# Moving SBUF tensors by multiples of 32 bytes in a cross-attention kernel

## The chip, the cores and the metric

The kernel runs on one core of a Trainium2 chip. The metric is the device time of one execution in microseconds (us). Three runs of the kernel before took 325.67 to 325.92 us, with a median of 325.76 us.

## The reference

```python
def ref(x, ctx, mask, Wq, Wk, Wv, Wo, gamma, beta):   # H = 8, D = 256, B = 8
    Q = (x @ Wq).reshape(B, -1, H, D).transpose(0, 2, 1, 3)        # x    8 x 256 x 256
    K = (ctx @ Wk).reshape(B, -1, H, D).transpose(0, 2, 1, 3)      # ctx  8 x 256 x 192
    V = (ctx @ Wv).reshape(B, -1, H, D).transpose(0, 2, 1, 3)
    score = einsum('bhqd,bhkd->bhqk', Q, K) / sqrt(D)
    attn = softmax(where(mask != 0, score, -inf))
    c = einsum('bhqk,bhkd->bqhd', attn, V).reshape(B, -1, H * D)
    out = c @ Wo + x
    return layernorm(out) * gamma + beta                            # eps 1e-5
```

## The kernel before, in words

The weights are folded once: A = Wq Wk^T and C = Wv Wo for each head (`fold_A`, `fold_C`, L316 to L355), so that a head costs only g = A^T x, scores = g^T ctx, t = ctx^T probs and out = t^T C. Context has 192 features, a lower part of 128 (L) and an upper part of 64 (U); the upper parts of two heads are packed into one tile.

Float32 accuracy comes from splitting every operand into a hi and a lo part, both `float32r`; each product is hi hi + hi lo + lo hi. All these matrix products go through `split_products` (L309 to L314), one `matmul` for each pair (stationary, moving). So each matmul on TensorE has two operands in SBUF, the stationary one, which a weight load brings in, and the moving one, which streams past. In the trace a matmul is written out<-moving,stationary.

The work is a pipeline of 32 steps (8 batches of 4 pairs of heads, `t` counts them). In `step` (L489 to L500) TensorE does four stages in this order:

- `scores(t)`: 20 matmuls, stationary `gL_hi`, `gL_lo`, `gU`, moving `ctxT_hi`, `ctxT_lo`, 256 columns each
- `query_products(t+1)`: 18 matmuls, stationary `A_hi`, `A_lo`, moving `xT_hi`, `xT_lo`, 256 columns
- `output_products(t-4)`: 18 matmuls, stationary `tL_hi`, `tL_lo`, `tU_hi`, `tU_lo`, moving `CL_hi`, `CL_lo`, `CU_hi`, `CU_lo`, 256 columns
- `context_products(t-3)`: 10 matmuls, stationary `ctxL_hi`, `ctxL_lo`, `ctxU`, moving `pT_hi`, `pT_lo`, 512 columns

ScalarE (ACT) makes the hi parts and the exponentials, VectorE (DVE) the lo parts of g and t, the maxima, the 32 x 32 transposes and the layer norm (its steps with j = 3 and j = 0 are the fullest, because add_residual, statistics, centre and normalise fall there), and GpSimd (POOL) divides the probabilities and makes the lo part of `pT`. The order on each engine is written out by hand; every dependence is a semaphore. The last steps differ: for `t` = 30, `places` (L125) puts the split t into tiles that are free by then, `xT_hi` and `xT_lo` as the lower stationary part and `gU` as the upper one.

SBUF tensors are allocated in the order of the `sb(...)` calls, one behind the other, each at the next address in a partition that is a multiple of 32 bytes. The first four (`wq_raw` to `wo_raw`) start at 16,512, a multiple of 128. All large tensors are multiples of 128 bytes long, so a start modulo 128 (the residue) is moved only by the small tensors that stand ahead: those of 8 or 16 bytes each take 32 bytes. Start addresses modulo 128 in the kernel before, and in the order that the change gives (worked out by this rule):

```
tensors                            before  changed
A_hi, A_lo                            0       0
gL_hi, gL_lo, gU                     64       0
tL_hi, tL_lo, tU_hi, tU_lo           32       0
ctxL_hi, ctxL_lo, ctxU               64      64
xT_hi, xT_lo, ctxT_hi, ctxT_lo       64      64
CL_hi, CL_lo, CU_hi, CU_lo            0      64
pT_hi, pT_lo (both buffers)          32      64
gamma, beta, ident, zeros             0      64
xT_raw, ctxT_raw, ctx_raw, mask*     64      64
x_res, neg_scores                    64      64
probs (both buffers)                 96      64
squares, pT_raw, tU_moved, tU        32      64
y, y_scaled, y_out                   32      64
```

All slices that a matmul takes start a multiple of 128 bytes behind the tensor's start, so these residues are those of the operands.

Of the kernel before, what the change touches and what calls it, by code (L numbers as in the profile page):

```python
# [8 lines left out]
F32R = mybir.dt.float32r  # L9
# [4 lines left out]
P = 128  # L14
B = 8
S = 256
KV = 256
# [7 lines left out]
UP = DL - P  # L25
PAIRS = H // 2
STEPS = B * PAIRS
QT = S // P
KT = KV // P
IT = DI // P  # L30
# [10 lines left out]
def attention_kernel(nc, xT, x, ctxT, ctx, mask, wqT, wkT, wvT, wo, gamma, beta, out, scratch):  # L41
    es = ExitStack()
    with es:
        def sb(name, shape, dt=F32):
            return es.enter_context(nc.sbuf_tensor(name, shape, dt))
# [11 lines left out]

        A_hi = sb("A_hi", [P, IT, PAIRS * PW], F32R)
        A_lo = sb("A_lo", [P, IT, PAIRS * PW], F32R)
        CL_hi = sb("CL_hi", [P, H, DI], F32R)  # L60
        CL_lo = sb("CL_lo", [P, H, DI], F32R)
        CU_hi = sb("CU_hi", [P, PAIRS, DI], F32R)
        CU_lo = sb("CU_lo", [P, PAIRS, DI], F32R)
        gamma_sb = sb("gamma_sb", [P, DI])
        beta_sb = sb("beta_sb", [P, DI])
        ident = sb("ident", [P, P])
        zeros = sb("zeros", [P, DI])
        eps_col = sb("eps_col", [P, QT])
        power_col = sb("power_col", [P, QT])

        xT_raw = sb("xT_raw", [P, IT, S])
        xT_hi = sb("xT_hi", [P, IT, S], F32R)
        xT_lo = sb("xT_lo", [P, IT, S], F32R)
        ctxT_raw = sb("ctxT_raw", [P, 2, KV])
        ctxT_hi = sb("ctxT_hi", [P, 2, KV], F32R)
        ctxT_lo = sb("ctxT_lo", [P, 2, KV], F32R)
        ctx_raw = sb("ctx_raw", [P, KT, DL])
        ctxL_hi = sb("ctxL_hi", [P, KT, P], F32R)
        ctxL_lo = sb("ctxL_lo", [P, KT, P], F32R)
        ctxU = sb("ctxU", [P, KT, 2 * UP], F32R)  # L80
        mask_raw = sb("mask_raw", [P, KV], I32)
        mask_low = sb("mask_low", [P, KV])
        mask_bias = sb("mask_bias", [P, KV])
        x_res = sb("x_res", [P, QT, DI])

        gL_hi = sb("gL_hi", [P, 2, S], F32R)
        gL_lo = sb("gL_lo", [P, 2, S], F32R)
        gU = sb("gU", [P, 2, S], F32R)
        neg_scores = sb("neg_scores", [P, 2 * QT, KV])
        neg_max = sb("neg_max", [P, 2 * QT])  # L90
        probs = [sb(f"probs{n}", [P, 2 * QT, KV]) for n in range(2)]
        row_sum = sb("row_sum", [P, 2 * QT])
        inv_sum = sb("inv_sum", [P, 2 * QT])
        squares = sb("squares", [P, SQUARES, 2 * QT, SQ])
        pT_raw = [sb(f"pT_raw{n}", [P, KT, ROWS, 2 * QT, SQ]) for n in range(2)]
        pT_hi = [sb(f"pT_hi{n}", [P, KT, 2, S], F32R) for n in range(2)]
        pT_lo = [sb(f"pT_lo{n}", [P, KT, 2, S], F32R) for n in range(2)]
        tL_hi = sb("tL_hi", [P, 2, S], F32R)
        tL_lo = sb("tL_lo", [P, 2, S], F32R)
        tU_moved = sb("tU_moved", [P, S])  # L100
        tU = sb("tU", [P, S])
        tU_hi = sb("tU_hi", [P, S], F32R)
        tU_lo = sb("tU_lo", [P, S], F32R)

        y = sb("y", [P, QT, DI])
        y_scaled = sb("y_scaled", [P, QT, DI])
        y_out = sb("y_out", [P, QT, DI])
        stats = sb("stats", [P, QT, 6])
        mean_var = sb("mean_var", [P, QT, 2])
        var_eps = sb("var_eps", [P, QT])  # L110
        rstd = sb("rstd", [P, QT])

# [999 lines left out]
```

How the kernel before makes its waits and increments, by code:

```python
        @block.sync  # L202
# [17 lines left out]
            def store_out(b):  # L220
                sp.wait_ge(y_out_done, QT * b + QT)
                sp.dma_start(batch_of(out, b), y_out[:]).then_inc(out_stored, 16)
# [24 lines left out]
            def load_ahead(b):  # L248
                sp.wait_ge(xT_split, b)
                load_xT(b)
                sp.wait_ge(ctxT_split, b)
                load_ctxT(b)
                sp.wait_ge(mask_lowered, b)
                load_mask(b)
# [1 line left out]
            def load_ctx_ahead(b):  # L257
                sp.wait_ge(ctx_split, 2 * b)
                load_ctx(b)
# [1 line left out]
            def load_residual(b):  # L262
                sp.wait_ge(out_bank_read, b + 1)
                load_x_res(b)
# [1 line left out]
            def carry_squares(t, j, raw_free=True):  # L267
                sp.wait_ge(squares_done, 2 * t + 2)
                sp.dma_start(scratch[j].rearrange("i c k jj r -> (i c) (k jj r)"),
                             squares[:].rearrange("p s n r -> p (s n r)")).then_inc(squares_stored, 16)
                sp.wait_ge(squares_stored, 16 * t + 16)
                if raw_free:
                    sp.wait_ge(pT_split, 2 * (t - 2) + 2)
                for jj in range(ROWS):
                    sp.dma_start(pT_raw[j % 2][SQ * jj:SQ * (jj + 1)].rearrange("c k i n r -> c k i (n r)"),
                                 scratch[j][:, :, :, jj, :].rearrange("i c k r -> c k i r")).then_inc(pT_in[j % 2], 16)
# [23 lines left out]
                sp.dma_start(out[B - 1][:, q, :], y_out[:, q, :]).then_inc(out_stored, 16)  # L303
            sp.wait_ge(out_stored, 16 * (B + QT))
```

## Time and profile before

| what | value |
|---|---|
| median of 3 runs | 325.76 us |
| the profiled execution's own time | 325.59 us |
| its span in the trace | 323.8 us |
| TensorE busy | 315.3 us, 97% |
| VectorE busy | 253.2 us, 78% |
| ScalarE busy | 222.4 us, 69% |
| GpSimd busy | 181.2 us, 56% |
| granted TensorE clock | full in all 40 slices |

How to read it: a span is the time from the first to the last instruction in the trace; the device time is longer by what lies around it. PE is TensorE's matmuls, PEld its weight loads. A matmul's recorded duration overlaps with the next one's, so what a matmul costs in a row of them is the distance from its start to the next one's start.

### The profile page before, as it was taken

The page shows a single profiled execution, that of the slowest core. Times are in us where ns is not written, and L with a number is a line of the kernel's source. Part 1 is how long each engine was busy: PE and PEld are TensorE (multiplying, and loading weights), DVE is VectorE, ACT ScalarE, POOL GpSimd, SP SyncE. Part 2 cuts the span into 40 slices and gives each one's busy share as a digit, 9 for nine tenths or more (in the row PEclk, how much of TensorE's full clock was granted, in tenths as well). Part 3 has the DMA queues.
Part 4 walks back from the last instruction along what each step waited for, and adds up shares of the span by engine and source line. Part 5 has one row for each costly group of instructions (what it writes and reads, how often), then busy time and mean ns, then how long its engine had stood idle before and what let it go on. Part 6 is the DMA issues. An engine that isn't in the chain of part 4 may idle for free.

```text
span 323.8 us, 7403 instructions
## 1 busy us (share of the span) xinstructions
PE 315.3 (97%) x2264; PEld 293.9 (91%) x2264; DVE 253.2 (78%) x721; ACT 222.4 (69%) x601; POOL 181.2 (56%) x183
## 2 busy tenths in 40 slices
PE   8999998999999999999999999999999999999992
PEld 6898887999999999999999999999999999998982
DVE  0457868777999779977997879977997789975685
ACT  2456668768867787668776797668766887777640
POOL 1122358457864487557855486548755686447211
PEclk9999999999999999999999999999999999999999
DMA  7995533464345453463345435364356525440100
GB/s 260 361 408 195 139 124 131 155 210 133 95 134 190 164 175 118 144 232 131 130 136 204 154 130 165 128 208 145 113 180 173 192 83 175 157 136 2 34 32 32
DMA packets 46910, 50.26 MB, mean 155 GB/s; under 512 B 3504, under 2 KB 37040, under 8 KB 46896
## 3 DMA queue, kind: packets, MB, share of 16 engines
q1 hardware_dynamic: 46608, 49.56, 46.0%
q10 hardware_dynamic: 288, 0.52, 0.6%
q8 instruction: 7, 0.11, 0.2%
q14 instruction: 7, 0.06, 0.1%
HBM read 32.24 MB, written 17.83 MB: 155 GB/s over the span
## 4 chain that ended last, share of the span: by engine, by line
PE 89%; DVE 3%; POOL 2%; DMA 2%; ACT 1%; issue 1%; SPq 1%; POOLq 0%; DVEq 0%
PE score_bank L312 23%; PE out_bank L312 19%; PE gL_bank L312 13%; PE tL_bank L312 13%; PE tU_bank L312 8%; PE gU_bank L312 7%; DMA wq_raw<-in_wqT 2%; PE tL_bank L346 1%; PE spare_bank L346 1%; PE tL_bank L328 1%; PE tU_bank L328 1%; POOL pT_lo L1016 1%; DVE tU L815 1%; PE tU_bank L352 1%; PE spare_bank L312 1%
## 5 line engine op out<-in xcount | busy, mean ns | idle before, releaser
L993 POOL TENSOR_TENSOR probs<-probs,inv_sum 128x512 f32<-128x512 f32 x64 | 66.8, 1044 | 87.8 <-DVE inv_sum L778 87.1
L590 ACT ACTIVATE probs<-neg_scores,neg_max 128x256 f32<-128x256 f32 x128 | 64.3, 504 | 31.8 <-DVE neg_max L767 31.7
L1016 POOL TENSOR_TENSOR pT_lo<-pT_raw,pT_hi 128x512 fp32r<-128x512 f32 x60 | 76.6, 1299 | 11.6 <-ACT pT_hi L547 11.6
L767 DVE CUSTOM_DVE_ANT_0 neg_scores<-score_bank,mask_bias 128x256 f32<-128x256 f32 x128 | 49.1, 420 | 7.4 <-PE score_bank L312 4.5
L547 ACT ACTIVATE tL_hi<-tL_bank 128x512 fp32r<-128x512 f32 x31 | 18.5, 598 | 38.4 <-PE tL_bank L312 38.4
L788 DVE STREAM_TRANSPOSE squares<-probs 128x512 f32<-128x512 f32 x60 | 42.3, 706 | 0.3
L715 DVE TENSOR_TENSOR tL_lo<-tL_bank,tL_hi 128x512 fp32r<-128x512 f32 x31 | 21.3, 687 | 23.2 <-ACT tL_hi L547 23.1
L312 PE MATMUL score_bank<-ctxT_hi,gU 128*128 128x256 f32 x128 | 36.5, 285 | 0.7 <-POOL ctxT_lo L1005 0.7
L312 PE MATMUL score_bank<-ctxT_hi,gL_lo 128*128 128x256 f32 x128 | 36.3, 283 | 0.0
L312 PE MATMUL score_bank<-ctxT_lo,gL_hi 128*128 128x256 f32 x128 | 36.2, 283 | 0.0
L312 PE MATMUL score_bank<-ctxT_hi,gL_hi 128*128 128x256 f32 x128 | 36.2, 283 | 0.0
L312 PE MATMUL score_bank<-ctxT_lo,gU 128*128 128x256 f32 x128 | 36.0, 281 | 0.0
L312 PE MATMUL gL_bank<-xT_hi,A_lo 128*128 128x256 f32 x128 | 35.4, 276 | 0.0
L312 PE MATMUL gL_bank<-xT_hi,A_hi 128*128 128x256 f32 x128 | 35.3, 276 | 0.0
L312 PE MATMUL gL_bank<-xT_lo,A_hi 128*128 128x256 f32 x128 | 35.3, 276 | 0.0
L547 ACT ACTIVATE pT_hi<-pT_raw 128x512 fp32r<-128x512 f32 x60 | 34.3, 622 | 0.0
L312 PE MATMUL out_bank<-CL_hi,tL_lo 128*128 128x256 f32 x118 | 33.3, 283 | 0.0
L312 PE MATMUL out_bank<-CL_lo,tL_hi 128*128 128x256 f32 x118 | 33.3, 282 | 0.0
L312 PE MATMUL out_bank<-CL_hi,tL_hi 128*128 128x256 f32 x118 | 33.1, 280 | 0.0
L715 DVE TENSOR_TENSOR gU<-gU_bank,gU 64x256 fp32r<-64x256 f32 x64 | 27.0, 422 | 2.1
L312 PEld LDWEIGHTS score_bank<-ctxT_hi,gU 128*128 128x128 f32 x128 | 24.3, 190 | 3.8 <-POOL ctxT_lo L1005 1.4
L815 DVE TENSOR_TENSOR tU<-tU_bank,tU_moved 64x256 f32<-64x256 f32 x62 | 26.0, 419 | 1.6 <-ACT tU_moved L631 0.6
(166 smaller groups left out, 949.7 us busy)
## 6 DMA issues: line engine op xcount, KB each, us to landing
scratch<-squares SPq DMA_DIRECT2D x30, 512.0 KB, 2.6
pT_raw<-scratch SPq DMA_DIRECT2D x120, 128.0 KB, 3.1
xT_raw<-in_xT SPq DMA_DIRECT2D x8, 256.0 KB, 4.4
ctxT_raw<-in_ctxT SPq DMA_DIRECT2D x8, 256.0 KB, 4.6
wo_raw<-in_wo SPq DMA_DIRECT2D x4, 512.0 KB, 13.9
x_res<-in_x SPq DMA_DIRECT2D x8, 256.0 KB, 3.2
out<-y_out SPq DMA_DIRECT2D x7, 256.0 KB, 2.7
wq_raw<-in_wqT SPq DMA_DIRECT2D x3, 512.0 KB, 7.4
```

The costliest lines, as they stand in the source:

```text
L312: ins = nc.tensor.matmul(into, stationary, moving, start=first and n == 0, stop=last and n == len(pairs) - 1, skip_group_check=shared)
L328: ins = nc.tensor.matmul(dst[:, i * DL:(i + 1) * DL], wq_raw[:, h * DT + d, i * P:(i + 1) * P], wk_raw[:, h * DT + d, :], start=d == 0, st ...
L346: ins = nc.tensor.matmul(lower[:, hh, :], wv_raw[:, h * DT + d, 0:P], wo_raw[:, h * DT + d, :], start=d == 0, stop=d == DT - 1)
L352: ins = nc.tensor.matmul(upper[hh * UP:(hh + 1) * UP, 0, :], wv_raw[:, h * DT + d, P:DL], wo_raw[:, h * DT + d, :], start=d == 0, stop=d = ...
L547: return nc.scalar.activation(dst, src, ACT.Copy)
L590: nc.scalar.activation(probs[j % 2][:, n, :], neg_scores[:, n, :], ACT.Exp, bias=neg_max[:, n:n + 1], scale=-1.0, accum_out=row_sum[:, n:n ...
L715: return nc.vector.tensor_tensor(dst, whole, hi.bitcast(F32), ALU.subtract)
L767: nc.vector.tensor_tensor_reduce(out=neg_scores[:, n, :], in0=score_bank[hh][:, q, :], in1=mask_bias[:], scale=-SCALE, scalar=3.0e38, op0= ...
L788: nc.vector.transpose(squares[:, :, rows, :].rearrange("p s n c -> p n s c"), probs[j % 2][:, rows, :].rearrange("p n (s c) -> p n s c", c ...
L815: nc.vector.tensor_tensor(tU[part, :], places("tU", t)[0][part, hh, :], tU_moved[part, :], ALU.add).then_inc(tU_summed, 1)
L993: nc.gpsimd.tensor_tensor(probs[j % 2][:, rows, :], probs[j % 2][:, rows, :], inv, ALU.mult) \
L1016: nc.gpsimd.tensor_tensor(pT_lo[j % 2][:, k].rearrange("p hh (q i r) -> p (hh q) i r", q=QT, i=ROWS), pT_raw[j % 2][:, k].rearrange("p i n ...
```

## The change

Only the order of the `sb(...)` calls changes; shapes, types, instructions, their order and their semaphores stay as they are.

```diff
         A_hi = sb("A_hi", [P, IT, PAIRS * PW], F32R)
         A_lo = sb("A_lo", [P, IT, PAIRS * PW], F32R)
+        gL_hi = sb("gL_hi", [P, 2, S], F32R)
+        gL_lo = sb("gL_lo", [P, 2, S], F32R)
+        gU = sb("gU", [P, 2, S], F32R)
+        tL_hi = sb("tL_hi", [P, 2, S], F32R)
+        tL_lo = sb("tL_lo", [P, 2, S], F32R)
+        tU_hi = sb("tU_hi", [P, S], F32R)
+        tU_lo = sb("tU_lo", [P, S], F32R)
+
+        eps_col = sb("eps_col", [P, QT])
+        power_col = sb("power_col", [P, QT])
+
+        ctxL_hi = sb("ctxL_hi", [P, KT, P], F32R)
+        ctxL_lo = sb("ctxL_lo", [P, KT, P], F32R)
+        ctxU = sb("ctxU", [P, KT, 2 * UP], F32R)
+
+        xT_hi = sb("xT_hi", [P, IT, S], F32R)
+        xT_lo = sb("xT_lo", [P, IT, S], F32R)
+        ctxT_hi = sb("ctxT_hi", [P, 2, KV], F32R)
+        ctxT_lo = sb("ctxT_lo", [P, 2, KV], F32R)
         CL_hi = sb("CL_hi", [P, H, DI], F32R)
         CL_lo = sb("CL_lo", [P, H, DI], F32R)
         CU_hi = sb("CU_hi", [P, PAIRS, DI], F32R)
         CU_lo = sb("CU_lo", [P, PAIRS, DI], F32R)
+        pT_hi = [sb(f"pT_hi{n}", [P, KT, 2, S], F32R) for n in range(2)]
+        pT_lo = [sb(f"pT_lo{n}", [P, KT, 2, S], F32R) for n in range(2)]
+
         gamma_sb = sb("gamma_sb", [P, DI])
         beta_sb = sb("beta_sb", [P, DI])
         ident = sb("ident", [P, P])
         zeros = sb("zeros", [P, DI])
-        eps_col = sb("eps_col", [P, QT])
-        power_col = sb("power_col", [P, QT])
...
         mean_var = sb("mean_var", [P, QT, 2])
+        neg_max = sb("neg_max", [P, 2 * QT])
+        row_sum = sb("row_sum", [P, 2 * QT])
+        inv_sum = sb("inv_sum", [P, 2 * QT])
         var_eps = sb("var_eps", [P, QT])
         rstd = sb("rstd", [P, QT])
```

The lines that are left out take each tensor that was moved away from its old place; `neg_max`, `row_sum` and `inv_sum` stood between `neg_scores`, `probs` and `squares`.

## Rows read from the trace of the kernel before

**Rows 1.** The page: span, TensorE's busy share, its granted clock in 40 slices.

```profile
span 323.8 us, 7403 instructions
...
PE 315.3 (97%) x2264; PEld 293.9 (91%) x2264; DVE 253.2 (78%) x721; ACT 222.4 (69%) x601; POOL 181.2 (56%) x183
...
PEclk9999999999999999999999999999999999999999
```

**Rows 2.** Chain of work that ended last, one step: start us, us, what.

```profile
195.51 2.39 PE score_bank L312 x20
197.90 0.68 PE gU_bank L312 x6
198.58 1.36 PE gL_bank L312 x12
199.94 2.16 PE out_bank L312 x18
202.10 0.94 PE tL_bank L312 x4
203.03 0.47 PE tU_bank L312 x2
...
204.43 2.39 PE score_bank L312 x20
```

**Rows 3.** Waits from 52 to 294 us: total us, times, longest.

```profile
PE score_bank L312 <- POOL ctxT_lo L1005: 0.7, 1, 0.7
```

**Rows 4.** TensorE's groups, each shape apart: busy us, mean ns of one.

```profile
L312 PE MATMUL score_bank<-ctxT_hi,gU 128*128 128x256 f32 x128 | 36.5, 285 | 0.7 <-POOL ctxT_lo L1005 0.7
...
L312 PE MATMUL gL_bank<-xT_hi,A_hi 128*128 128x256 f32 x128 | 35.3, 276 | 0.0
...
L312 PE MATMUL out_bank<-CL_hi,tL_lo 128*128 128x256 f32 x118 | 33.3, 283 | 0.0
...
L312 PE MATMUL tL_bank<-pT_hi,ctxL_hi 128*128 128x512 f32 x62 | 24.9, 401 | 0.2 <-issue 0.2
```

**Rows 5.** Timeline of TensorE near the end: start us, us, matmul.

```profile
301.41 0.28 PE L312 MATMUL spare_bank<-CL_lo,tL_hi 128*128 128x256 f32 x1
...
302.60 0.28 PE L312 MATMUL out_bank<-CL_hi,tL_lo 128*128 128x256 f32 x1
...
313.47 0.28 PE L312 MATMUL spare_bank<-CL_hi,xT_hi 128*128 128x256 f32 x1
...
315.39 0.28 PE L312 MATMUL out_bank<-CU_hi,gU 128*128 128x256 f32 x1
```

**Rows 6.** Busy time of each engine in steps j=3 and j=0 (us, instructions).

```profile
186.40:204.30 17.90, 17.90 (x134) 16.96 (x133) 15.86 (x46) 13.70 (x38) 13.83 (x15) 1.00 0.43 143
```

**Rows 7.** Timeline of VectorE over steps j=3 and j=0: start us, us, instruction.

```profile
187.02 0.69 DVE L715 TENSOR_TENSOR tL_lo<-tL_bank,tL_hi 128x512 fp32r<-128x512 f32 x1 [1.39 <-ACT tL_hi L547]
187.97 0.42 DVE L767 CUSTOM_DVE_ANT_0 neg_scores<-score_bank,mask_bias 128x256 f32<-128x256 f32 x1 [0.25 <-PE score_bank L312]
...
203.26 0.69 DVE L715 TENSOR_TENSOR gL_lo<-gL_bank,gL_hi 128x512 fp32r<-128x512 f32 x1
...
205.36 0.68 DVE L715 TENSOR_TENSOR tL_lo<-tL_bank,tL_hi 128x512 fp32r<-128x512 f32 x1
```

**Rows 8.** Timeline of TensorE: the first matmul that reads the lo part from rows 7.

```profile
204.75 0.28 PE L312 MATMUL score_bank<-ctxT_hi,gL_lo 128*128 128x256 f32 x1
```

**Rows 9.** Chain of work that ended last, the first steps.

```profile
19.24 2.60 PE score_bank L312 x20
...
34.04 2.59 PE score_bank L312 x20
...
49.06 2.05 POOL probs L993 x2
```

**Rows 10.** Chain of work that ended last, the end.

```profile
305.02 0.60 ACT tL_hi L547
...
316.13 1.36 PE spare_bank L312 x9
```

More of the change, by code:

```diff
@@ L67, in attention_kernel @@
         zeros = sb("zeros", [P, DI])
-        eps_col = sb("eps_col", [P, QT])
-        power_col = sb("power_col", [P, QT])
         xT_raw = sb("xT_raw", [P, IT, S])
-        xT_hi = sb("xT_hi", [P, IT, S], F32R)
-        xT_lo = sb("xT_lo", [P, IT, S], F32R)
         ctxT_raw = sb("ctxT_raw", [P, 2, KV])
-        ctxT_hi = sb("ctxT_hi", [P, 2, KV], F32R)
-        ctxT_lo = sb("ctxT_lo", [P, 2, KV], F32R)
         ctx_raw = sb("ctx_raw", [P, KT, DL])
-        ctxL_hi = sb("ctxL_hi", [P, KT, P], F32R)
-        ctxL_lo = sb("ctxL_lo", [P, KT, P], F32R)
-        ctxU = sb("ctxU", [P, KT, 2 * UP], F32R)
         mask_raw = sb("mask_raw", [P, KV], I32)
@@ L84, in attention_kernel @@
         x_res = sb("x_res", [P, QT, DI])
-        gL_hi = sb("gL_hi", [P, 2, S], F32R)
-        gL_lo = sb("gL_lo", [P, 2, S], F32R)
-        gU = sb("gU", [P, 2, S], F32R)
         neg_scores = sb("neg_scores", [P, 2 * QT, KV])
-        neg_max = sb("neg_max", [P, 2 * QT])
         probs = [sb(f"probs{n}", [P, 2 * QT, KV]) for n in range(2)]
-        row_sum = sb("row_sum", [P, 2 * QT])
-        inv_sum = sb("inv_sum", [P, 2 * QT])
         squares = sb("squares", [P, SQUARES, 2 * QT, SQ])
         pT_raw = [sb(f"pT_raw{n}", [P, KT, ROWS, 2 * QT, SQ]) for n in range(2)]
[L96 to L99, printed above, removed]
         tU_moved = sb("tU_moved", [P, S])
         tU = sb("tU", [P, S])
-        tU_hi = sb("tU_hi", [P, S], F32R)
-        tU_lo = sb("tU_lo", [P, S], F32R)
         y = sb("y", [P, QT, DI])
```

## The prediction

> **What bounds the kernel now.** I read the page first: TensorE is busy 97% of the span at the full granted clock in every slice, 2.4 GHz, the higher of its two levels [rows 1]. Busy TensorE is not proof of a bound, so the chain of waits came next. From 52 to 294 us it is TensorE alone: one step is 20 score matmuls in 2.39 us, 6 + 12 query matmuls in 2.04, 18 output matmuls in 2.16 and 10 context matmuls from 202.10 to 204.43, 2.33, together 8.92 us [rows 2]. Then the waits: in this stretch TensorE waited 0.7 us once, at its start, and never again [rows 3]. So nothing but the distance from one matmul to the next sets 27 steps of the pipeline (t = 4 to 30), about 241 us. A change that touches no instruction can matter only through that distance.
>
> **What the distance depends on now.** Each stage divided by its count gives ns per matmul: scores 2.39/20 = 119.5, query 2.04/18 = 113.3, output 2.16/18 = 120, context 2.33/10 = 233 for twice the columns [rows 2]. Three stages have the same shape, yet one is 6 to 7 ns faster; the mean durations say the same, 285 and 283 against 276 ns [rows 4]. Put the residues of the SBUF map beside it: query has stationary 0, moving 64 (64 apart), scores 64 and 64 (0 apart), output 32 and 0 (32 apart), context 64 and 32 (32 apart). That may be the stage and not the address, so I looked for one stage with two addresses. The end has it: for t = 30 the split t lies in `xT` and `gU` at residue 64, with C at 0 as always. Those output matmuls, 17 distances from 313.47 to 315.39, take 113 ns; the same form with `tL` at 32, 10 distances from 301.41 to 302.60, takes 119 [rows 5]. Same helper, shape, moving tiles and banks, another stationary address. I take it that 64 apart is the fast case whichever of the two stands at 0, and that 0 and 32 apart both cost 6 to 7 ns at 256 columns.
>
> One rule speaks against all of this. The Trainium skill (TensorE: Matmul & The Clock Gate, Step-by-step: what each phase is for) says that TensorE reads its moving operand and its weights through two independent ports, so that loading the next weights takes nothing from the running matmul. By it addresses would not matter and the sum would be zero, 325.8 us; by the rows above it is not. The trace disagrees with it by those 6 to 7 ns [rows 2, 5].
>
> **The change part by part.**
>
> Scores go from 0 to 64 apart (stationary 0, moving 64: just what query has). 20 x 113.3 ns = 2.27 us against 2.39: -0.12 a step.
>
> Output goes from 32 to 64 apart, again 0 and 64: 18 x 113.3 = 2.04 against 2.16: -0.12 a step.
>
> Query keeps 0 and 64: nothing.
>
> Context goes from 32 apart (stationary 64, moving 32) to 0 apart, both at 64. No row shows 512 columns at 0 or 64 apart, so I bound it. Below: an undisturbed 256-column matmul takes 113.3 ns and 256 further columns at 2.4 GHz 106.7, so 220 ns, 2.20 us a step (-0.13). Above: twice a score matmul at 0 apart, 2 x 120 = 240, 2.40 us (+0.07). Inside: 220 plus the 6.7 ns that 0 apart costs the scores is 226.7; twice the fast query matmul is also 226.7. I take that, 2.27 us, -0.06 a step. Unchanged at 233 is a serious alternative, since at 256 columns 0 and 32 apart cost the same.
>
> The other tiles: `ident` and `zeros` move from 0 to 64, for 16 transposes and the warming only, nothing to speak of. The operands of GpSimd's lo part of `pT` were at one residue (32) and are again (64). Several ScalarE and VectorE operands change residue (`probs` 96 to 64, `squares` 32 to 64, `tU` stays away from its hi part by 64 instead of 0). The trace shows no price for that on these engines; what hides it is the slack before TensorE's waits, below. DMA destinations shift likewise, under the same cover.
>
> Step: 8.92 - 0.12 - 0.12 - 0.06 = 8.62 us, -0.30.
>
> **Does it all lie on the path?** Steps 4 to 30: 27 x 0.30 = 8.1 us. Before them the chain holds the scores of t = 0 to 2 but then goes through GpSimd (pT lo, ctx, probs) until 52 us [rows 9]: 3 x 0.12 = 0.36 saved, and the scores of t = 3 hidden. After them, t = 31: scores 0.12, 30 output matmuls ahead of 305 us at 6.7 ns = 0.20, two context blocks 0.12; at 305.02 the chain passes to ScalarE and VectorE until 316.13, when TensorE has 9 last output matmuls [rows 10], 0.06. In the stretch between, 12 matmuls with `xT` as stationary become 0 apart and lose 12 x 6.7 = 0.08 us, but TensorE is not what the chain follows there; uncovered it would cost that 0.08. Sum 8.1 + 0.36 + 0.44 + 0.06 = 9.0 us. Against the profiled execution's own 325.59 that is 316.6; the median is 0.17 above that execution, so **316.8 us**.
>
> **Do the others keep up?** The fullest pair of steps for VectorE is j = 3 and j = 0: 15.86 us busy in 17.90 [rows 6]. From its tL_lo at 187.02 to the one at 205.36 it takes 18.34 us, with three waits inside of 0.25 to 0.29 (the first is shown), 0.82 in all, so 17.5 us without waiting [rows 7]. The pair will last 2 x 8.62 = 17.24. So VectorE comes out of it up to 0.3 us late, and catches up in the next two steps, each of which has some 2 us of room. What TensorE waits for there is gL_lo: done at 203.26 + 0.69 = 203.95, first read at 204.75, so 0.80 us early [rows 7, 8]. Even if none of VectorE's waits shrank, that becomes 0.80 - 0.60 - 0.03 = 0.17; if they all do, up to 0.99. Close, but no wait. ScalarE and GpSimd, 13.70 and 13.83 us in the pair [rows 6], are further away.
>
> **Rivals.**
>
> *Context takes another value.* At 233 ns, unchanged: 9.0 less 29 x 0.06 = 7.3 us saved, 318.5. At 240: 29 x 0.07 more is lost, 320.5. At 220: 29 x 0.07 more is gained, 314.8. For unchanged speaks the equality of 0 and 32 at 256 columns; for 220 speaks that its moving tile comes from 32 to a start like the fast stages', so that part of what it pays now may belong to the start and not to the distance.
>
> *VectorE becomes the bound* in the fullest pairs, because its instructions are slower at their new addresses or its late pair does not recover. Then a pair lasts 17.5 instead of 17.24, or with the order's gaps about 17.6: 7 pairs x 0.36 = 2.5 us given back, 319.3. Against: the slack of gL_lo, and that TensorE waits on nothing now. It decides from 0.17 to 0.99 us of growth over some 16 us of VectorE work, 1 to 6%.
>
> *Nothing changes*, 325.8: the 6 to 7 ns belong to the stage and the case at the end is an accident. This is the rule of the ports named above. Against: it would have to explain 113 and 119 ns for one form of instruction [rows 5].
>
> *Slower*: context at one residue collides on every access of the weight load and not once a matmul. The rest gains 7.3 us, and some 290 context matmuls are on the path, so it decides from 7.3/290 = 25 ns each, 258 instead of 233. At 265 ns: 327.8 us. Against: the scores are at 0 apart too and pay 7 ns, for as many weights; the load does not grow with the columns.
>
> **How the numbers follow.** Forecast, context near 227 and the rest as reckoned: 0.45, own range 315.6 to 317.7. Context unchanged up to 240, 317.7 to 320.5: 0.22. Context toward 220, 314.4 to 315.6: 0.14. VectorE as bound, about 319.3: 0.08. No change: 0.05. Slower: 0.04. Left over: 0.02. From 314.5 to 320.5 about 0.87 is held. I keep that range because its ends are the bounds of the context price. A measurement of this kernel can tell about 0.2%, 0.65 us, from no change; all cases but the last three are faster than that: faster 0.90, same 0.06, slower 0.04.
>
> **What will show it.** In the chain of the changed kernel a step should read scores 2.27, query 2.04, output 2.04, context 2.27, step starts 8.62 apart. Score and output groups should have a mean of 276 ns, as query. The 12 matmuls on `xT` near the end should rise from 113 to 120 ns: the one place where the change makes a pair worse, and so the check on the mechanism. No new wait of TensorE before 294 us, and gL_lo still ahead of its reader in steps j = 0. I am wrong if scores or output stay at 119 ns, if context leaves 220 to 240, or if TensorE begins to wait for VectorE.

## The result, and the profile after

The changed kernel takes 325.05 us (median of 18 runs, 324.65 to 325.78), the kernel before 325.81 us (18 runs, 325.59 to 326.13): a ratio of 0.9977, 95% interval 0.9970 to 0.9984. It is faster, but by 0.76 us, where 9 were forecast. The mean granted clock is 0.999 in both profiled executions. For two experiments (e9 and e13, below) single runs are told, since they fall into groups 8 to 10 us apart at the same granted clock (0.995 to 1.000), and that is the finding.

The page of the changed kernel: span, TensorE's busy share, its granted clock.

```profile
span 322.8 us, 7403 instructions
...
PE 313.6 (97%) x2264; PEld 293.2 (91%) x2264; DVE 253.1 (78%) x721; ACT 222.2 (69%) x601; POOL 181.0 (56%) x183
...
PEclk9999999999999999999999999999999999999999
```

TensorE still sets the time and waits as rarely as in [rows 3]; its waits from 52 to 294 us:

```profile
PE score_bank L314 <- POOL ctxT_lo L1007: 0.7, 1, 0.7
```

Two steps of the chain of work that ended last (start us, us, what), against [rows 2]:

```profile
61.56 2.27 PE score_bank L314 x20
63.82 0.68 PE gU_bank L314 x6
64.50 1.36 PE gL_bank L314 x12
65.86 2.04 PE out_bank L314 x18
67.90 0.93 PE tL_bank L314 x4
...
70.19 2.35 PE score_bank L314 x20
72.55 0.71 PE gU_bank L314 x6
73.26 1.41 PE gL_bank L314 x12
74.67 2.12 PE out_bank L314 x18
76.79 0.93 PE tL_bank L314 x4
...
79.10 0.94 PE score_bank L314 x8
```

These two steps do the same work with the same addresses. (`gU_bank` and `gL_bank` are the two parts of query.) The first, from 61.56, is the forecast step: scores 2.27, query 2.04, output 2.04, 8.63 us in all. The second, from 70.19, has scores 2.35 (2.36 by the matmuls' starts), query 0.71 + 1.41 = 2.12, output 2.12, together 8.91, and all later steps are like it. Query, whose residues did not change, went from 113.3 to 117.7 ns a matmul. Context takes 2.31 us in the second kind of step and 2.29 in the first, where [rows 2] have 2.33.

The groups of TensorE (busy us, mean ns of one), against [rows 4]:

```profile
L314 PE MATMUL score_bank<-ctxT_hi,gU 128*128 128x256 f32 x128 | 36.3, 283 | 0.7 <-POOL ctxT_lo L1007 0.7
L314 PE MATMUL gL_bank<-xT_hi,A_hi 128*128 128x256 f32 x128 | 35.8, 280 | 0.0
...
L314 PE MATMUL out_bank<-CL_hi,tL_lo 128*128 128x256 f32 x118 | 32.9, 279 | 0.0
L314 PE MATMUL tL_bank<-pT_hi,ctxL_hi 128*128 128x512 f32 x62 | 24.6, 398 | 0.3 <-issue 0.3
```

Scores fell from 285 to 283 ns here and output from 283 to 279, but query rose from 276 to 280. Near the end, the 12 output matmuls with `xT` as the stationary part, which are now 0 apart, were to rise from 113 to 120 ns. Nine distances of the timeline (start us, us, matmul), against [rows 5]:

```profile
312.68 0.28 PE L314 MATMUL spare_bank<-CL_hi,xT_hi 128*128 128x256 f32 x1
...
313.76 0.28 PE L314 MATMUL spare_bank<-CU_hi,gU 128*128 128x256 f32 x1
```

1.08/9 = 120 ns: that check came out (of the twelve distances only the first, 113 ns, did not rise). VectorE did not become the bound either. Its lo part of g in the fullest steps, and the first matmul that reads it, from two timelines, against [rows 7, 8]:

```profile
202.63 0.69 DVE L717 TENSOR_TENSOR gL_lo<-gL_bank,gL_hi 128x512 fp32r<-128x512 f32 x1
```

```profile
204.10 0.28 PE L314 MATMUL score_bank<-ctxT_hi,gL_lo 128*128 128x256 f32 x1
```

It ends at 203.32 and is read at 204.10, 0.78 us later, as before (0.80).

### The profile page after: what moved, and what is told of

It is laid out like the page before. It is cut to its first block, busy times and chain, and to the rows that moved or that the text cites. A ratio compares the mean times of both kernels' runs of the same rounds, so it can differ in the third digit from the quotient of the medians.

```text
span 322.8 us, 7403 instructions
## 1 busy us (share of the span) xinstructions
PE 313.6 (97%) x2264; PEld 293.2 (91%) x2264; DVE 253.1 (78%) x721; ACT 222.2 (69%) x601; POOL 181.0 (56%) x183
## 4 chain that ended last, share of the span: by engine, by line
PE 89%; DVE 3%; POOL 2%; DMA 2%; ACT 1%; issue 1%; SPq 1%; POOLq 0%; DVEq 0%
PE score_bank L314 23%; PE out_bank L314 19%; PE gL_bank L314 14%; PE tL_bank L314 12%; PE tU_bank L314 8%; PE gU_bank L314 7%; DMA wq_raw<-in_wqT 2%; PE tL_bank L348 1%; PE spare_bank L348 1%; PE tL_bank L330 1%; PE tU_bank L330 1%; POOL pT_lo L1018 1%; DVE tU L817 1%; PE tU_bank L354 1%; PE spare_bank L314 1%
```

## The experiments

All kernels keep the order of the changed one, or of the one before where it is said, and move groups of tiles by unused tensors between the `sb(...)` calls, each of 32, 64 or 96 bytes a partition. What stands behind the last unused tensor has its old residue again and lies 128 or 256 bytes further on (e15 moves all that follows by 64). The traces show no addresses; the residues follow from the order of allocation. Theory A, formed after the result: matmuls 64 apart have two rhythms (a steady distance from one start to the next), 113.3 ns and 117.7 ns, and stay in the one in which they enter. Theory B: the address itself slowed query (`xT` and what stands beside it moved). The table gives the steady step, in us for each stage, summed from matmul starts in each trace; "a / b" are the residues of stationary and moving tiles. The time is the median, the ratio is to the kernel before on the same chip.

| kernel | scores | query | output | context | step | time, ratio [95%] |
|---|---|---|---|---|---|---|
| before | 2.39 (64/64) | 2.04 (0/64) | 2.16 (32/0) | 2.34 (64/32) | 8.93 | 325.8 |
| changed | 2.36 (0/64) | 2.12 (0/64) | 2.12 (0/64) | 2.31 (64/64) | 8.91 | 325.05, 0.9977 [0.9970, 0.9984] |
| e12, before, scores alone | 2.36 (0/64) | 2.12 | 2.13 (32/0) | 2.34 (64/32) | 8.94 | 325.96, 1.0005 [0.9995, 1.0014] |
| e4, before, output alone | 2.38 (64/64) | 2.04 | 2.11 (64/0) | 2.34 (64/32) | 8.87 | 324.24, 0.9946 [0.9930, 0.9961] |
| e1, changed, scores back | 2.40 (64/64) | 2.04 | 2.04 (0/64) | 2.30 (64/64) | 8.79 | 321.81, 0.9870 [0.9829, 0.9911] |
| e2, changed, context 32 apart | 2.36 | 2.12 | 2.12 | 2.33 (64/32) | 8.93 | 325.88, 0.9997 [0.9981, 1.0012] |
| e3, changed, context 64 apart | 2.35 | 2.12 | 2.12 | 2.31 (64/0) | 8.90 | 325.13, 0.9971 [0.9955, 0.9987] |
| e5, changed, gU at 64 | 2.34 | 2.12 | 2.12 | 2.32 | 8.89 | 324.45, 0.9960 [0.9946, 0.9974] |
| e6, changed, gL_lo at 64 | 2.36 | 2.06 | 2.04 | 2.29 | 8.75 | 321.00, 0.9864 [0.9836, 0.9893] |
| e7, all 0/64 | 2.27 or 2.36 | 2.04 or 2.12 | 2.04 or 2.12 | 2.29 to 2.34 (0/64) | 8.83 (mean) | 322.64, 0.9904 [0.9888, 0.9921] |
| e8, e7 with scores 64/64 | 2.39 | 2.04 | 2.04 | 2.29 (0/64) | 8.76 | 321.34, 0.9867 [0.9847, 0.9887] |

**One part alone, on the kernel before.** e12 moves gL and gU from 64 to 0, e4 moves tL and tU from 32 to 64:

```diff
+        pad0 = sb("pad0", [P, 16])        # e12
         gL_hi = sb("gL_hi", [P, 2, S], F32R)
...
+        pad1 = sb("pad1", [P, 16])
         neg_scores = sb("neg_scores", [P, 2 * QT, KV])
```
```diff
+        pad0 = sb("pad0", [P, 8])         # e4
         tL_hi = sb("tL_hi", [P, 2, S], F32R)
...
+        pad1 = sb("pad1", [P, 24])
         tU_moved = sb("tU_moved", [P, S])
...
+        pad2 = sb("pad2", [P, 8])
         tU_hi = sb("tU_hi", [P, S], F32R)
...
+        pad3 = sb("pad3", [P, 24])
         y = sb("y", [P, QT, DI])
```

> The kernel before with only gL_hi, gL_lo and gU moved from residue 64 to 0, so scores 64 apart; query 64 apart, output and context 32 apart as before. Two-rhythm theory: what the scores gain the query stage can lose, since nothing puts it back into the fast rhythm: after the context stage both run at 118 ns (as in the changed kernel), step 2.36 + 2.12 + 2.16 + 2.33 = 8.97 us, about 327; if context happens to hand over the fast rhythm, both at 113, step 8.80, about 322. Address theory (each stage has its own price): scores 113, query untouched 113, 322.5.

> The kernel before with only tL_hi, tL_lo, tU_hi, tU_lo moved from residue 32 to 64 (C stays at 0, so output is 64 apart); scores 0 apart, context 32 apart as before. Theory A: output follows a query stage that is in the fast rhythm and takes it over: 113 ns, step 8.93 - 0.12 = 8.81 us, time about 322.3. Theory B (118 is what such a stage gets at its addresses): output 113 or 118 ns, no telling; at 118 step 8.89 us, time about 324.7.

e12's chain of work, one steady step:

```profile
196.22 2.36 PE score_bank L314 x20
198.58 0.70 PE gU_bank L314 x6
199.29 1.41 PE gL_bank L314 x12
200.70 2.13 PE out_bank L314 x18
```

Only the scores' stationary tiles moved. Scores won 0.03 us and query, untouched, lost 0.08: the whole kernel gained nothing. So the price of a stage depends on what runs ahead of it. Theory B and the forecast both fall here, because `xT` and `A` stand exactly where they stood before.

e4 is a miss for theory A: 324.2 us where it said 322.3. The query stage keeps its 113 ns, but output, which should have taken that over, does not. From the timeline of e4's output stage (start us, us, matmul):

```profile
199.13 0.28 PE L316 MATMUL out_bank<-CL_hi,tL_hi 128*128 128x256 f32 x1
...
200.42 0.28 PE L316 MATMUL out_bank<-CL_hi,tL_lo 128*128 128x256 f32 x1
...
200.89 0.28 PE L316 MATMUL out_bank<-CU_hi,tU_hi 128*128 128x256 f32 x1
...
201.23 0.39 PE L316 MATMUL tL_bank<-pT_hi,ctxL_hi 128*128 128x512 f32 x1
```

The first eleven distances, from 199.13 to 200.42, are 117 to 119 ns, the last three, from 200.89 to 201.23, are 113 to 114, and it is so in each step. So two things go against "stay in the one in which they enter": the rhythm went from 113 to 118 ns at the border of two stages, and from 118 back to 113 inside a stage whose residues are the same throughout. At the border the sides change (query has 0/64, output 64/0), which they do not in e1, next; that this is the reason is not shown.

**The scores put back.** e1 is the changed kernel with gL and gU at 64, where they meet `ctxT` 0 apart:

```diff
+        pad0 = sb("pad0", [P, 16])
         gL_hi = sb("gL_hi", [P, 2, S], F32R)
...
+        pad1 = sb("pad1", [P, 16])
         tL_hi = sb("tL_hi", [P, 2, S], F32R)
```

> The changed kernel with gL and gU back at residue 64, so 0 apart from ctxT; query, output (64 apart) and context (0 apart) as changed. Theory A (two rhythms: matmuls 64 apart run at 113 ns or at 118 ns, by how the run is entered, and a stretch at 0 apart hands over to the fast one, as in the kernel before): scores 119 to 120 ns, query and output back at 113 ns, context about 231; step 2.39 + 2.04 + 2.04 + 2.31 = 8.78 us, time about 322. Theory B (query is slow because of the new absolute addresses of xT and its neighbours): query and output stay at 118 ns, step 2.39 + 2.12 + 2.12 + 2.31 = 8.94 us, time about 326.

The chain of e1, a steady step from its query stage on:

```profile
195.78 0.69 PE gU_bank L316 x6
196.46 1.36 PE gL_bank L316 x12
197.82 2.04 PE out_bank L316 x18
...
202.16 2.40 PE score_bank L316 x20
```

Query is back at 0.69 + 1.36, with `xT` and all of its neighbours at their residues of the changed kernel, 128 bytes further on, and `A` not moved at all; output gets its forecast 2.04. 321.8 us, as theory A had it and theory B (326) had not. Making one stage slower by 0.05 us made two others faster by 0.08 each.

**The context stage.** e2 and e3 move pT to residue 32 and 0 (an unused tensor ahead of `pT_hi`, one ahead of `gamma_sb` to restore what follows):

> The changed kernel with pT at residue 32 (context 32 apart, as in the kernel before), the other three stages 64 apart. Both theories: context back to about 233 to 234 ns. Theory A: the way in is now another one, so the three stages sit at 113 or at 118 ns, all of them the same: step 6.35 + 2.33 = 8.68 us and 319 us, or 6.59 + 2.33 = 8.92 us and 325.8 us. Theory B: 118 ns, 325.8 us.

> The changed kernel with pT at residue 0, so that all four stages are 64 apart. Theory A: context at 220 to 227 ns if no collision is left, and the three other stages all at 113 (about 8.60 us a step, 317 us) or all at 118 ns (about 8.83 us, 323 us). Theory B: 118 ns in the three stages, 323 us.

Context costs 2.33 us at 32 apart, 2.31 at 0 and 2.31 at 64. The distance hardly matters there, and no context stage of any trace has a mean of 220 ns a matmul (the lowest is 228.5). The three other stages stay at 118 in both, and both times for e3 (317 or 323) were missed, since they counted on a faster context.

**How little is enough.** e5 and e6 put single tiles of the scores at 64:

> The changed kernel with gU alone at residue 64: 8 of the 20 score matmuls are 0 apart, two of every five; all else as changed. If a few matmuls at 0 apart, the last of them three before the end of the stage, are enough to hand over to the fast rhythm: query and output 113 ns, scores about 116, step 2.32 + 2.04 + 2.04 + 2.30 = 8.70 us, about 320 us. If the run of 0 apart has to be long or has to reach up to the query stage: 118 ns, about 325 us.

> The changed kernel with gL_lo alone at residue 64: every fifth score matmul is 0 apart, the last one right ahead of the query stage. If the last matmul ahead of a run 64 apart decides its rhythm: query and output 113 ns, scores about 115, step 2.30 + 2.04 + 2.04 + 2.30 = 8.68 us, about 319 us. If one matmul does not do it: 118 ns, about 325 us.

With gU at 64 (two of five score matmuls) it failed, with gL_lo at 64 (the last of every five, the last one of all right ahead of query) it worked: 321.0 us, though its scores did not fall to 115 ns as expected but stayed at 118. The chain of e6:

```profile
195.46 0.69 PE gU_bank L316 x6
196.15 1.36 PE gL_bank L316 x12
197.51 2.04 PE out_bank L316 x18
...
201.84 2.36 PE score_bank L316 x20
```

**One side for all.** e7 puts ctxL and ctxU at 0, so that every stationary tile is at 0 and every moving one at 64; e8 is e7 with gL and gU at 64 (the same kind of padding, 64 bytes ahead of `ctxL_hi` and of `xT_hi`).

> The changed kernel with ctxL_hi, ctxL_lo and ctxU at residue 0 and pT at 64: all four stages 64 apart, and now every stationary tile at 0 and every moving one at 64, so that no border between stages puts a load and a stream at one residue. Two-rhythm theory: nothing disturbs the rhythm any more, so all stages of all steps after the last wait at 52 us keep what they began with: 113 and 220 to 227 ns (about 8.6 us a step, 317 us) or 118 ns and about 230 (8.9, 325), and the time of single runs may fall into two groups. Rival, that the context stage of 512 columns itself throws the rhythm off whatever its address: 118 ns as in the changed kernel, 325 us.

> The faster version found so far (gL and gU at residue 64, so scores 0 apart) with ctxL_hi, ctxL_lo and ctxU at residue 0, context 64 apart. Two-rhythm theory: scores 120, query and output 113 as there; context enters from the fast rhythm at 64 apart and should take 220 to 227 ns instead of 230: step 2.40 + 2.04 + 2.04 + 2.25 = 8.73 us, about 320.5. Rival, context does not depend on the address: 230 ns, 321.8.

The score stages of five steps in a row, from the chain of e7:

```profile
61.48 2.36 PE score_bank L316 x20
...
70.42 2.36 PE score_bank L316 x20
...
79.32 2.27 PE score_bank L316 x20
...
87.96 2.36 PE score_bank L316 x20
...
96.89 2.36 PE score_bank L316 x20
```

2.36, 2.36, 2.27, 2.36, 2.36: every third step is fast, in all three stages, over the whole trace. Within a step the rhythm holds for all 56 matmuls of 256 columns; it changes only across the 10 of 512. So the rival in e7's expectation is right that context throws the rhythm off whatever its address, and wrong that it always ends in the slow one. In e8 the scores at 0 apart restore the fast one each time; its context stayed at 229 ns, so there too the rival was right.

**No 512-column matmuls.** If context changes the rhythm, the clean test has none. e9 writes each as two of 256 columns, one for each head, with the layout of e7:

```diff
+            def halves(into, pairs, first=True, last=True):
+                for n, (stationary, moving) in enumerate(pairs):
+                    for hh in range(2):
+                        ins = nc.tensor.matmul(into[:, hh, :], stationary, moving[:, hh, :],
+                                               start=first and n == 0 and hh == 0,
+                                               stop=last and n == len(pairs) - 1, skip_group_check=True)
+                return ins
...
-                    lower = split_products(tL[:], [(ctxL_hi[:, k, :], lo[:, k])], first=False, last=end)
+                    lower = halves(tL, [(ctxL_hi[:, k, :], lo[:, k])], first=False, last=end)
```

The kernels from e9 on use it at each of the context products and differ in residues:

| kernel with halves | scores | query | output | context | step | time, ratio [95%] |
|---|---|---|---|---|---|---|
| e9, all 0/64 | 2.36 | 2.12 | 2.12 | 2.36 | 8.95 | single runs 316.93, 324.55, 326.44, 326.58 |
| e10, gL_lo at 64 | 2.36 | 2.12 | 2.12 | 2.36 | 8.96 | 326.85, 1.0032 [1.0019, 1.0044] |
| e11, context 64/64 | 2.27 | 2.04 | 2.04 | 2.40 | 8.75 | 321.39, 0.9867 [0.9851, 0.9884] |
| e13, tU at 64 (6 matmuls) | 2.36 | 2.12 | 2.12 | 2.36 | 8.95 | five runs 318.1 to 318.5, five 326.5 to 326.8 |
| e14, tL at 64 (12) | 2.36 | 2.12 | 2.14 | 2.36 | 8.97 | 326.65, 1.0028 [1.0016, 1.0039] |
| e15, all 0/0 (76) | 2.37 | 2.13 | 2.15 | 2.40 | 9.05 | 329.43, 1.0109 [1.0092, 1.0126] |
| e16, tL and tU at 64 (18) | 2.27 | 2.04 | 2.16 | 2.27 | 8.73 | 320.59, 0.9842 [0.9825, 0.9858] |
| e17, gL and gU at 64 (20) | 2.40 | 2.04 | 2.04 | 2.27 | 8.75 | 321.00, 0.9849 [0.9832, 0.9865] |

> The layout with every stationary tile at residue 0 and every moving one at 64, and each context product of 512 columns written as two of 256, one for each head (20 matmuls for 10, the same weights loaded twice). Now all 76 matmuls of a step have one shape and one distance. Two-rhythm theory, in which the 512-column matmuls are what changes the rhythm from step to step: no change of rhythm any more after the last wait near 52 us; either all at 113.3 ns, 8.61 us a step and 317 us, or all at 117.8 ns, 8.95 us and 326 us. Rival (the rhythm drifts for another reason, such as other engines): the pattern of 113 and 118 steps goes on.

The profiled execution of e9 took 326.44 us. Its chain, one step:

```profile
196.13 2.36 PE score_bank L316 x20
198.49 0.71 PE gU_bank L316 x6
199.20 1.41 PE gL_bank L316 x12
200.61 2.12 PE out_bank L316 x18
```

From 61 to 286 us its distances are 116 to 120 ns, the mean 117.8, and none is 113. Another run of this same program took 316.93 us. The forecast of the two-rhythm theory was 317 or 326. That run has no trace; that it is the one at 113 ns throughout follows from the time alone (27 steps x 76 x 4.4 ns = 9.0 us, measured 9.5), and the run of 324.55 us is not explained further.

> As the run with halves and one side for all, but gL_lo at residue 64, so that every fifth score matmul is 0 apart and the query stage begins in the fast rhythm in each step. Two-rhythm theory: scores about 118 ns as in the earlier run with gL_lo at 64, the other 56 matmuls 113.3: 2.36 + 6.35 = 8.71 us a step, about 320. Rival: context does not get faster by halves (230 ns a pair): 8.74 us, 321.

> The changed kernel's layout unaltered, with the context products in halves of 256 columns, which are then 0 apart at the size of the scores. Two-rhythm theory: the context stage is now the one that pays 120 ns (20 x 120 = 2.40 us) and that hands over the fast rhythm to the next step, scores, query and output 113.3 ns: 2.27 + 2.04 + 2.04 + 2.40 = 8.75 us, about 321. Rival: 118 ns in the three others, 2.36 + 2.12 + 2.12 + 2.40 = 9.0 us, about 328.

e10 failed: the single matmuls 0 apart that had done it in e6 did not here. The two kernels differ in two things, the halves and the context stage's stationary tiles (at 64 in e6, at 0 in e10). e11 is the changed kernel's own layout, residue for residue, and it gains 4.4 us on the kernel before. Its chain:

```profile
87.90 2.27 PE score_bank L314 x20
90.17 0.68 PE gU_bank L314 x6
90.85 1.36 PE gL_bank L314 x12
92.21 2.04 PE out_bank L314 x18
94.25 0.96 PE tL_bank L418 x8
...
96.65 2.27 PE score_bank L314 x20
```

Now context is a run of 20 matmuls of 256 columns, 0 apart, at 120 ns (0.96 for 8), and the other 56 are at 113.3. So the residues of the change are good for what the forecast expected of three stages; its 512-column context stage is what spoils them.

**What hands over the fast rhythm.** The first three of these take 6, 12 and all 76 matmuls to 0 apart, the last two 18 and 20, each in one unbroken run:

> The layout with one side for all and halves, but tU_hi and tU_lo at residue 64: the last 6 output matmuls of a step are 0 apart in one unbroken run, the other 70 are 64 apart. If an unbroken run, even a short one, hands over the fast rhythm (the single ones among 64 apart did not in the run with gL_lo): 70 x 113.3 ns + 6 x 120 = 8.65 us a step, about 318, and single runs agree. If six are too few to settle: 118 ns, 8.96 us, 326.5, or single runs that differ by up to 9 us.

> As the run before, but tL_hi and tL_lo are at 64 and tU at 0: 12 matmuls in an unbroken run, 64 at 64 apart. If a long run is what it takes: 64 x 113.3 + 12 x 120 = 8.69 us, about 319.5, single runs agree. If it is the last matmuls ahead of the context stage that matter and not the length: no telling, 118 ns, 326.5.

> Halves, and every operand of the four stages at residue 0: all 76 matmuls of a step 0 apart. If 0 apart has one rhythm only, 120.0 ns however it is entered: 9.12 us a step, about 331, and single runs agree within 0.5 us. If it has two as well, single runs differ as with the layout 64 apart.

> Halves, one side for all but the stationary tiles of the output stage: tL and tU at residue 64, an unbroken run of 18 matmuls 0 apart, 58 at 64 apart. If length is what counts (12 were too few, 20 were enough in the kernel before and in the run with context 0 apart): context, scores and query at 113.3, output about 120: 58 x 113.3 + 18 x 120 = 8.73 us a step, about 321. If the place counts and not the length: 58 x 117.8 + 18 x 119 = 8.97 us, 327.

> As the run before with the 0 apart run moved to the scores stage (gL and gU at 64, tL and tU at 0): 20 matmuls 0 apart right ahead of the query stage, 56 at 64 apart. Scores 120, all else 113.3 as after the scores of the kernel before: 8.74 us a step, about 321, single runs agree. If the halves of context spoil it: 118 ns in the others, 8.99 us, 327.

Six: in half of the runs, and that half is at the 318 us that was expected (its ratio alone is 0.977, but a run gets it or not; the trace is of the other half, so that the 318 us runs had the fast rhythm follows from their time alone). Twelve: in the trace once, in the first full step. The next twelve were entered in the fast rhythm and came out in the slow one (context at 118), and so it stayed. The chain of e14 in a steady step, the larger part of query and the output:

```profile
199.31 1.41 PE gL_bank L318 x12
200.72 2.14 PE out_bank L318 x18
```

Eighteen: always, in four runs of four, at the place where twelve had failed. The chain of e16:

```profile
195.46 1.36 PE gL_bank L318 x12
196.82 2.16 PE out_bank L318 x18
198.97 0.91 PE tL_bank L422 x8
...
201.24 2.27 PE score_bank L318 x20
```

Output pays 2.16, the rest is at 113.3. Twenty in the scores stage: the same, so both places do. And 76: single runs agree within 0.63 us (328.87 to 329.50), close to what was expected of one rhythm, but the mean of the stages is 118.4 to 119.8 ns and not 120.0 everywhere; in scores and query of e15 the distances repeat as 120, 119, 115, 117, 122, in context most are 120. So 0 apart has more than one rhythm too. e15 took 9.05 and not 9.12 us a step.

## Why the prediction was wrong

The step that failed is "I take it that 64 apart is the fast case", and with it "Query keeps 0 and 64: nothing". The forecast priced each stage by its own two residues. The price is 113.3 or 117.7 ns at the same residues, by what ran before, and the fast price of query in the kernel before rested on the scores stage ahead of it, 20 matmuls at 0 apart (e12 takes only that away and query goes from 2.04 to 2.12 us; e1 gives it back and query returns to 2.04). The change took away just that.

- *Bound by TensorE's distances, other engines keep up*: right. No new wait; gL_lo is 0.78 us early.
- *Scores -0.12, output -0.12*: right for the one step at 61.56 us, wrong for the 26 others of the 27: -0.03 and -0.04. e16 and e17 show both values where the rhythm is held.
- *Query 0*: +0.08 a step. This is the term that eats the gain of both: -0.03 - 0.04 + 0.08 = 0.01.
- *Context -0.06 (227 ns)*: -0.03, 231 ns. Its bounds held, its mechanism did not: distance is worth some 0.02 us a step (e2, e3), and what matters for it is that it changes the rhythm (e7, e9).
- *Sum*: step 8.91 for 8.62. One step of 8.63 and 26 that gain about 0.02 make 0.3 + 0.5 = 0.8 us, of 8.1 forecast. Ahead of these 27 steps 0.05 us was saved of 0.36, since query lost there too, and behind them 0.13 of 0.5, in the two traces, whose spans are 1.0 us apart; the medians are 0.76 apart.
- *The control at the end* of the trace before ([rows 5], 113 against 119) was sound as far as it went: 32 apart and 64 apart did differ there, and its twelve matmuls rose to 120 as forecast when they came to be 0 apart. That this check came out is no support for the sum: it was one sample of a stage 64 apart, and by luck in the fast rhythm (a context stage ran ahead of it; what put it there is not shown). All query stages of the trace before were too, since each came right behind a run 0 apart.
- *The rival of no change* had 0.05. The reason given with it, the two independent ports of the Trainium skill (TensorE: Matmul & The Clock Gate, Step-by-step: what each phase is for), would make addresses indifferent, and there the measurement decides against it: among the kernels with halves nothing but addresses differs, and they take 320.6 to 329.4 us (e16, e15). That the whole came out near that rival's 325.8 is a balance of -0.03, -0.04, -0.03 and +0.08 us a step, not its mechanism. Whether the weight load itself takes from the stream, no run isolates.

What is shown: the two rhythms (e1, e7, e12), that 256-column matmuls as a rule hold the one they are in while sides and distance stay (e7 within each step, e9 throughout; the output stage of e4 is an exception), that the rhythm changed across the 512-column ones and did not when these were halved (e7 against e9's profiled execution), that unbroken runs of 18 and 20 at 0 apart gave the fast one in every steady step of seven traces (before, e1, e4, e8, e11, e16, e17); across a wait, as at 52 us in e11, they need not. Open too is why e6 works with single matmuls and e10 does not, why output changes its rhythm inside the stage in e4, why 12 fail in the steady steps and 6 in half of the runs, and whether 18 is a matter of length; there is one kernel for each. Address bits above the residue were not varied by themselves: where an unused tensor shifts what follows by 128 or 256 bytes, they change too. Free of that are the changed kernel against e11, e7 against e9, steps within one trace, and the query stages of e4 and e12, whose own tiles did not move. The version to keep is e16, or, with unused tensors alone, e6 (321.0) or e1 (321.8), which has the unbroken run.

## What to carry to other kernels

In this kernel, where TensorE sets the time and weights are reloaded for each matmul, start addresses modulo 128 were worth 1.3 to 1.4% by themselves (e1, e6) and 1.6% together with halves (e16). Look at them in a kernel like it, but price them by a trace of the whole order of stages, not one stage at a time. A stage that looks fast may owe it to a slow one ahead of it; before removing the slow one, look at what its neighbours do when they enter from elsewhere. Look at the first steps of a trace too, and at single runs: one step at 8.63 among 8.91, or runs in two groups, show a state that a median hides.

## What the runs showed of the hardware that was not expected

- Back-to-back matmuls of 256 columns with their own 128-column weight load, both float32r, at the full granted clock: 113.3 or 117.7 ns from start to start with the operands 64 bytes apart modulo 128, in the same program and at the same addresses (e7, every third step). 120 ns when 0 apart for a stage of 20 (e11, e17), 118.4 to 119.8 when all four stages are 0 apart (e15).
- In e9 the profiled execution held one of them for 240 us; single runs of this program took from 316.93 to 326.58 us.
- Two matmuls of 256 columns with a weight load each took 2 x 113.3 = 226.6 ns in the fast rhythm, one of 512 columns 228 to 234 on average: in the fast rhythm the halves cost nothing more (context 2.27 us in e16 against 2.29 in e8, both with residues 0/64). In the slow one they do: 2 x 117.8 = 236 ns, 2.36 us in e9.
